# Queries of step 6 made ahead of that step's scores, and one chunk of keys made behind the weighted values, in a decoder layer on one core

## What is computed

```python
x = _layernorm(x + _L0_attn_ref(x, Wq, Wk, Wv, Wo))              # self attention, 16 heads of 16
qh, kh, vh = heads(x @ Wq), heads(context @ Wk), heads(context @ Wv)
sim = jnp.einsum('hid,hjd->hij', qh, kh) * SCALE
mean = jnp.mean(sim, axis=-1, keepdims=True)
sim = (sim - mean) * 1.5 + mean
out = jnp.einsum('hij,hjd->hid', jax.nn.softmax(sim, axis=-1), vh)
x = _layernorm(x + merge(out) @ Wout + bout)
x = _layernorm(x + _L0_ffn_ref(x, W1, b1, W2, b2))               # 256 -> 1024 -> 256, ternary weights
```

## Time and profile before

| | |
|---|---|
| median of 3 runs | 2304.46 us (2302.53 to 2307.41) |
| the profiled execution | 2306.85 us, its span 2305.1 us |
| mean granted clock of TensorE | 0.996 |
| TensorE busy (matrix products) | 2252.5 us, 98% |
| VectorE busy | 2020.4 us, 88% |
| GpSimd busy | 1898.6 us, 82% |
| ScalarE busy | 1865.1 us, 81% |
| DMA, mean share of the queues' packets in the span | 6.5% |

### The profile page before, as it was taken

How to read it: one execution, slowest core, us unless ns; L and a number is a source line. 1 busy time by engine, 2 the same in 40 slices (tenths; PEclk the granted TensorE clock), 3 DMA queues, 4 the chain that set the end, 5 groups by cost and what they waited for, 6 DMA issues and landing times.

```text
span 2305.1 us, 61948 instructions
## 1 busy us (share of the span) xinstructions
PE 2252.5 (98%) x26078; PEld 1980.7 (86%) x26078; DVE 2020.4 (88%) x2241; ACT 1865.1 (81%) x2224; POOL 1898.6 (82%) x1153
## 2 busy tenths in 40 slices
PE   7998999999999999999999999999999999999998
PEld 4557998899889998899888998899889998998886
DVE  7878988988889888988898898988899888898876
ACT  4357888888888888888878888888888888888855
POOL 8675888888878888888888898888878888899953
PEclk8999999999999999999999999999999999999999
DMA  7400000000000000000000000000000000010220
GB/s 201 158 32 21 6 4 13 4 7 6 11 6 4 7 13 4 6 4 7 13 4 5 6 13 4 6 4 7 13 4 6 4 6 6 4 47 7 90 79 33
DMA packets 34837, 50.44 MB, mean 22 GB/s; under 512 B 2304, under 2 KB 27392, under 8 KB 34560
## 3 DMA queue, kind: packets, MB, share of 16 engines
q1 hardware_dynamic: 34560, 46.46, 6.5%
HBM read 30.99 MB, written 15.47 MB: 20 GB/s over the span
## 4 chain that ended last, share of the span: by engine, by line
PE 71%; POOL 15%; DVE 6%; issue 4%; ACT 3%; POOLq 0%; DVEq 0%; ACTq 0%
PE psum L420 26%; POOL e_lo L1618 12%; PE psum L452 9%; PE psum L445 9%; PE psum L450 5%; PE psum L448 5%; PE psum L567 4%; PE psum L557 4%; POOL e_hi L1612 3%; DVE run_max L1082 3%; ACT ring L847 2%; PE psum L693 2%; PE psum L740 1%; PE psum L529 1%; PE psum L574 1%
## 5 line engine op out<-in xcount | busy, mean ns | idle before, releaser
L1618 POOL TENSOR_TENSOR e_lo<-ring,e_hi 128x1024 f16<-128x1024 f32 (+1 forms) x665 | 1388.8, 2103 | 196.4 <-ACT ring L862 160.8
L1082 DVE TENSOR_TENSOR run_max<-psum,run_max 128x1024 f16<-128x1024 f32 (+1 forms) x616 | 737.9, 1198 | 183.5 <-ACT ring L847 180.3
L847 ACT ACTIVATE ring<-psum 128x1024 f32<-128x1024 f32 (+1 forms) x672 | 673.7, 1003 | 180.0 <-PE psum L420 104.8
L1103 DVE SCALAR_TENSOR_TENSOR ring<-ring,psum 128x1024 f32<-128x1024 f32 (+1 forms) x672 | 792.5, 1186 | 0.7 <-PE psum L660 0.7
L420 PE MATMUL psum<-qx_hi,k_hi 128*128 128x256 f16 x2632 | 718.0, 273 | 15.5 <-DVE run_max L1082 9.1
L420 PE MATMUL psum<-qx_hi,k_lo 128*128 128x256 f16 x2632 | 717.8, 273 | 0.0
L420 PE MATMUL psum<-qx_lo,k_hi 128*128 128x256 f16 x2632 | 717.7, 273 | 0.0
L452 PE MATMUL psum<-v_main,e_lo 128*128 128x129 f16 x4032 | 711.4, 220 | 0.0
L862 ACT ACTIVATE ring<-ring 128x1024 f32<-128x1024 f32 (+1 forms) x672 | 696.1, 1036 | 1.3 <-DVE ring L1103 0.7
L445 PE MATMUL psum<-v_main,e_hi 128*128 128x257 f16 x2016 | 550.4, 273 | 1.3 <-POOL e_lo L1618 1.3
L450 PE MATMUL psum<-v_main,e_hi 128*128 128x128 f16 x2016 | 446.9, 222 | 0.0
(11 more groups left out here) (203 smaller groups left out, 3171.2 us busy)
## 6 DMA issues: line engine op xcount, KB each, us to landing
o_scratch<-o_buf SPq DMA_DIRECT2D x56, 128.0 KB, 1.9
raw<-o_scratch SPq DMA_DIRECT2D x14, 512.0 KB, 4.4
stage<-in_ctxT SPq DMA_DIRECT2D x6, 500.0 KB, 3.9
stage<-in_ctxT SPq DMA_DIRECT2D x12, 250.0 KB, 4.9
w_scratch<-wall SPq DMA_DIRECT2D x1, 2304.0 KB, 10.9
wall<-w_scratch SPq DMA_DIRECT2D x6, 384.0 KB, 3.2
x<-in_xT SPq DMA_DIRECT2D x4, 448.0 KB, 6.6
res<-in_x SPq DMA_DIRECT2D x1, 1792.0 KB, 17.6
```

Of the source, the lines that this page charges most:

```text
L847: a.activation(ring[:, f % SLOTS, 0:n], pair(f)[:, 0:n], ACT.Copy).then_inc(s_kept, 1)
L1082: ins = v.tensor_tensor(run_max[:, 0:n], pair(f)[:, 0:n], run_max[:, 0:n], ALU.max)
L1103: v.scalar_tensor_tensor(slot, slot, LIFT, psum[:, 6, 0:QB].unsqueeze(1).broadcast_to([P, t, QB]), ALU.add, ALU.subtract).then_inc(s_sub, 1)
L1618: g.tensor_tensor(e_lo[f % NEL][:, 0:n], slot, e_hi[f % NEH][:, 0:n], ALU.subtract).then_inc(s_lo, 1)
```

## The change

Two edits, each on all engines that it concerns.

1. `ahead_of(n, s)` holds at step 6 of the blocks with qb 5 and 6 where queries are made: 14 places (the first seven heads, two each). There the queries' product stands ahead of the scores on TensorE, the high half ahead of `keep_scores` on ScalarE, and the low half ahead of `running_max` on VectorE.
2. `behind` gets the pair (5, 0): the product of key chunk 2 stands behind the weighted values, and its high half behind the full exponential: 7 places.

```diff
         def behind(n, s):
 
-            return 0 <= n < NBLK - NQB and (n % NQB, s) in ((4, 10), (5, 1), (5, 4), (5, 10), (6, 1), (6, 4))
+            return 0 <= n < NBLK - NQB and (n % NQB, s) in ((4, 10), (5, 0), (5, 1), (5, 4), (5, 10), (6, 1), (6, 4))
+
+        def ahead_of(n, s):
+
+            return s == 6 and n >= 0 and n % NQB in (5, 6) and side_of(n, s) is not None
...
                     target, ts = n + ahead // NGRP, ahead % NGRP
+                    if ahead_of(n, s):
+                        side(n, s, past, number)
                     if target < NBLK:
                         scores(n * NGRP + ahead, past * NQB * NGRP, past * HEAD_SIDES, ts, target % 2)
                     task = side_of(n, s)
                     if task is not None:
                         if task[0] == "t":
                             transposes(n_at, number)
-                        elif not behind(n, s):
+                        elif not behind(n, s) and not ahead_of(n, s):
                             side(n, s, past, number)
...
+                    if ahead_of(n, s):
+                        high_half(n, s, number)
                     if f + LEAD < NF_ALL:
                         keep_scores(f + LEAD)
                     task = side_of(n, s)
-                    if task is not None and task[0] != "t" and not behind(n, s):
+                    if task is not None and task[0] != "t" and not behind(n, s) and not ahead_of(n, s):
                         high_half(n, s, number)
...
+                    if ahead_of(n, s):
+                        halves += 1
+                        low_half(n, s, halves)
                     if f + LEAD < NF_ALL:
                         running_max(f + LEAD)
                     if s == MAX_S + 2 and 0 <= ready < NF_ALL:
                         subtract(ready)
                     if task is not None:
-                        if task[0] != "t":
+                        if task[0] != "t" and not ahead_of(n, s):
                             halves += 1
                             low_half(n, s, halves)
                         number += 1
```

## The result

The change is slower: 2312.46 us against 2307.68 us for the kernel before (19 runs of each), a ratio of 1.002 with a 95% interval of 1.0013 to 1.0027, or +4.6 us (3.0 to 6.2). The kernel before measures 3.2 us more here than in the three runs that the prediction had, so of the distance between 2312.46 and the forecast of 2294.0, 3.2 us is the level of the runs and the rest is the change. Rival 1 had +5.4. Runs of one kernel differ by about 5 us with their mean granted clock; taken at one clock, the change measures 2312.76 (16 runs) against 2307.36 (28 of the runs made beside the experiments) at up to 0.997, and 2307.72 (3 runs) against 2302.73 (3 runs) at 0.999, or +5.4 and +5.0.

The account below looks back on a forecast made before the run. TensorE, busy 98% of the span, was taken as the bound. Terms -8.6 - 1.8 + 0 = -10.4 us took the profiled 2306.85 to 2296.4, less 2.4 to the runs' median: 2294.0 us, range 2292.0 to 2310.5.

Parts of the forecast that it names:

- Rival 1: GpSimd's cast goes ahead of VectorE's first fold in all 14 places: +5.4 us, 2309.8 us; chance 0.35.
- What bounds the kernel: TensorE, kept busy by matrix products for 98% of the span; only its idle time or added work can move the time.
- part 1's direct effect: Queries made ahead of the scores at step 6, qb 5 and 6: the 14 stalls at step 7 go, -8.6 us.
- rows 2: Profile waits before: scores for the queries' low half 14 times, 6.4 us; row-maxima spread late 8 times, no releaser, 2.3 us.
- I take the fold as first, by the row of the same pair: At the 14 places VectorE's first fold was taken to beat GpSimd's cast, though the cast was computed about 0.01 us ahead.
- K: The end of ScalarE's keeping of the step 6 scores, from which the cast's and first fold's starts were computed.
- turning point: Difference between cast and first fold starts at which the one holding up the other changes; put between -0.03 and +0.02 us.
- rows 7: Trace rows before, 8 places: same fold and cast, cast 0.02 us behind; fold took 0.41, cast was stretched to 1.29.
- What is late next: After the stalls, VectorE's chain to the row-maxima spread on TensorE decides; fold first, late spreads at 8 places go, -1.8 us.
- Part 2: Key chunk 2 behind the weighted values at step 0 of qb 5, 7 places: taken as 0, bounds 1.0 us either way.
- Rival 2: The qb 5 and qb 6 places fall differently on who goes first: about -2.5 us, 2302 us; chance 0.10.
- rival 3: Queue order isn't what delays the queries, or their product waits for its PSUM bank: 2304.5 us; chance 0.08 with others.

Follow-up runs that it names:

- the fill: The changed kernel with a tiny GpSimd fill of 128x4 numbers right ahead of the cast at the 14 places: ratio 0.9945 to the kernel before.
- the wait alone: The kernel before, with GpSimd's cast made to wait for VectorE's second fold at the 14 places: ratio 0.9990, attention time -2.0 us.
- the same wait put in all blocks: The changed kernel with GpSimd's cast waiting for the second fold at step 6 of every block: ratio 1.0029 to the kernel before.

## Why the prediction was wrong

**What bounds the kernel** and **part 1's direct effect** held: the 14 waits of rows 2 are gone.

**The step that failed** is the choice in "I take the fold as first, by the row of the same pair". The order of the two starts was worked out rightly, K + 1.01 against K + 1.02 forecast, K + 1.01 against K + 1.03 measured. The turning point, which I put anywhere between -0.03 and +0.02, was then set to the losing side of -0.01 for no better reason than that rows 7 came from the same two instructions. The runs give in its place: the cast 0.01 to 0.02 ahead wins (14 of 14 places), 0.02 behind it loses (14 of 14 with the fill, and the 8 of rows 7). So the turning point lies between 0.01 ahead and 0.02 behind, and the forecast's -0.01 stood on the cast's side of it: the first fold took 1.30 us and not 0.41. The Trainium skill, SBUF — State Buffer, section "Who interferes with whom", says that whichever issues first wins, and the trace after agrees, 0.02 ahead and 1.30 for 0.41. The prediction had that rule and its 2309.8 beside the forecast (as "the second rival's", which is rival 1's); taken at its word it was right.

**What is late next**: right in both branches. With the cast first, the row maxima were forecast 0.38 later, and came 0.39 later; rival 1 had +5.4 (its own 14 x 0.38 is 5.3) against +5.2 in the trace and +4.6 (3.0 to 6.2) in the runs. With the fold first, the forecast's -8.6 - 1.8 = -10.4 became -11.0 as soon as a fill turned the order round. The sum of the forecast is the time of a kernel 0.04 us away from this one at 14 places. Its 1.8 was nearly right by luck. It took the 8 unnamed waits of rows 2 for waits at qb 5 and 6; by their starts four lie at qb 6 and four at qb 4, which the change doesn't touch. From the start of the last weighted value of step 8 to the scores of step 9, a block without delay takes 0.17 us. Before, four qb 5 blocks took 0.20 to 0.29 more, four at qb 6 0.22 to 0.23 more and three at qb 6 0.07 more: 2.0 us together, the gain that the wait alone brought.

**Part 2**: taken as 0, measured +0.1.

**Rival 2** (the two kinds of place fall differently) did not occur; **rival 3** is out by the waits that went.

**The range** ended at 2310.5 on a base of 2304.46. Rival 1 lay inside it, by 0.7 us; the three runs of the base stood 3.2 us under the median of more runs, and the range had allowed for such a spread around the forecast (2.5 either way) but not around rival 1 at its upper end. The step from the profiled execution down to the median, 2.4 us, is what made the base low: 28 runs of the kernel before at a mean clock of 0.996 or 0.997 lie between 2306.0 and 2308.3, like the profiled 2306.85 at 0.996, and 2306.85 + 5.4 = 2312.3 is within 0.3 us of the measured median.

## What to carry to other kernels

Where two engines share a lock, the order of two starts can be worth more than the edit: work out both starts from what each hangs on, and if they lie within some hundredths, don't choose by the likelier side, but put a cheap instruction or a wait in that fixes the order the way you want it. Give the loser as little delay as it takes: 0.04 us kept the whole gain, 0.9 us lost a quarter of it, and the same wait put in all blocks turned the gain into a loss. A stall removed from the bounding engine is had only as far as the engine that feeds it next has slack; compare the slot of its next wait with the end of that chain first.

## What the runs showed of the hardware

- A difference of 0.03 to 0.04 us in the start of one GpSimd instruction moved the end of VectorE's second fold by about 2 us: 1164.61 - 1161.17 = 3.44 behind the first fold's start in the change, 1158.56 - 1157.09 = 1.47 with the fill.
- A GpSimd fill recorded as running when the fold began (1157.07 to 1157.17, the fold at 1157.09) did not hold the fold back by more than 0.01 (0.42 for 0.41): of GpSimd's instructions the cast and the subtraction did, both of which read SBUF.
- A 0.10 us fill moved the instruction behind it by 0.04, and the two records overlap (1157.07 to 1157.17, and from 1157.11).
- The granted clock of TensorE in the first 100 us differs from one execution to the next (0.93 to 1.00), and with it the start of the attention, by up to 5.5 us. That is more than the effect of the change.
